# Choice, scores, feature rows and the last LayerNorm of a vision tower moved between its attention loop and its expert loop

## The reference, cut to what matters

```python
h = h + attn(layernorm(h), w_qkv, b_qkv, w_proj, b_proj)      # 32 images x 65 tokens x 64
x = layernorm(h)                                              # "the second LayerNorm"
logits = einsum('bsd,ed->bse', x, gate_w)                     # 64 experts a token
top_logits, indices = top_k(logits, 6)
scores = softmax(top_logits)
xW = einsum('bsd,bskde->bske', x, lattice_weights[indices])
lattice_out = einsum('bske,bsk->bse', xW, scores)
proj = lattice_out @ out_w.T + out_b
y = x + proj
h = h + (y - mean(y)) * rsqrt(var(y) + 1e-5) * ln_g + ln_b
```

## Time and profile before

| what | us |
|---|---|
| median of 3 runs | 1084.4 (1083.52 to 1084.65) |
| the profiled execution | 1083.5 |
| its span in the trace | 1081.6 |
| attention loop, first scores to the end of the last value products | 836.8 to 928.0 |
| from there to the first broadcast of the expert loop | 928.0 to 952.5 |
| expert loop, to the end of the last expert products | 952.5 to about 1070.5 |
| output of the last block | to 1081.6 |

### The profile page before, as it was taken

How to read it: one execution, slowest core, us unless ns; L and a number is a source line. 1 busy time by engine, 2 the same in 40 slices (tenths; PEclk the granted TensorE clock), 3 DMA queues, 4 the chain that set the end, 5 groups by cost and what they waited for, 6 DMA issues and landing times.

```text
span 1081.6 us, 36566 instructions
## 1 busy us (share of the span) xinstructions
PE 979.3 (91%) x17004; PEld 623.9 (58%) x17004; DVE 617.2 (57%) x773; ACT 397.9 (37%) x522; POOL 151.4 (14%) x158
## 2 busy tenths in 40 slices
PE   4899899999989999999899899999899898688885
PEld 3667667657656533676567567656216687533342
DVE  2268457737833221587278357633143677769887
ACT  2432233224223486232332233224675567411100
POOL 6000000000000000000000000020010765334421
PEclk9999999999999899999999999999999899779998
DMA  5220230032022201310220220030001000000000
GB/s 196 93 78 3 69 90 17 3 105 67 4 90 102 59 6 40 109 30 3 93 78 4 78 87 9 4 100 10 14 14 44 2 2 1 2 1 1 2 11 10
DMA packets 25918, 46.78 MB, mean 43 GB/s; under 512 B 9949, under 2 KB 11000, under 8 KB 25125
## 3 DMA queue, kind: packets, MB, share of 16 engines
q1 hardware_dynamic: 24118, 42.47, 12.5%
q0 software_dynamic: 1456, 1.63, 0.6%
q10 hardware_dynamic: 192, 0.33, 0.1%
HBM read 30.25 MB, written 10.89 MB: 38 GB/s over the span
## 4 chain that ended last, share of the span: by engine, by line
PE 74%; DVE 12%; issue 5%; ACT 3%; POOL 3%; DMA 2%; SPq 1%; POOLq 0%; DVEq 0%
PE PSALL L1296 22%; PE PSALL L1264 7%; PE PSALL L1158 5%; PE PSALL L1287 5%; PE PSALL L1373 5%; PE PSALL L1239 4%; PE PSALL L1172 4%; PE PSALL L526 3%; PE PSALL L1383 3%; DVE WORK L1503 3%; PE PSALL L427 2%; DVE WORK L1003 2%; PE PSALL L513 2%; DVE WORK L1522 2%; PE PSALL L1135 2%
## 5 line engine op out<-in xcount | busy, mean ns | idle before, releaser
L1522 DVE STREAM_TRANSPOSE WORK<-PSALL 128x1024 f32<-128x1024 f32 x128 | 152.5, 1230 | 252.9 <-PE PSALL L1264 252.9
L1296 PEld LDWEIGHTS PSALL<-EW,WORK 128*64 128x64 f32 x4096 | 221.8, 138 | 72.8 <-issue 48.3
L1296 PE MATMUL PSALL<-EW,WORK 128*64 128x128 f32 x4096 | 247.6, 276 | 14.0 <-DVE WORK L1522 13.7
L1422 ACT ACTIVATE X<-PSALL,TABLES 128x1024 f32<-128x1024 f32 x128 | 141.8, 1114 | 307.2 <-PE PSALL L1296 307.2
L1503 DVE STREAM_TRANSPOSE WORK<-PSALL 128x1024 f32<-128x1024 f32 x84 | 104.3, 1242 | 32.8 <-PE PSALL L1158 30.9
L324 POOL DMA_DIRECT2D WORK<-MIXED x32 | 17.6, 550 | 670.5 <-ACT MIXED L1413 557.2
L1404 ACT COPY SPEC<-PSALL 128x400 f32<-128x400 f32 x64 | 54.4, 850 | 136.6 <-PE PSALL L1172 132.9
L1172 PEld LDWEIGHTS PSALL<-TABLES,WORK 128*64 128x64 f32 x2000 | 67.1, 138 | 48.8 <-DVE WORK L1503 31.4
L1003 DVE TENSOR_TENSOR WORK<-PSALL,X 128x832 f32<-128x832 f32 x80 | 79.3, 1017 | 16.8 <-PE PSALL L513 15.3
L1172 PE MATMUL PSALL<-TABLES,WORK 128*64 128x64 f32 x2000 | 80.7, 228 | 7.9 <-DVE WORK L1503 3.8
L1456 ACT ACTIVATE WORK<-PSALL,B 128x1024 f32<-128x1024 f32 x64 | 67.8, 1110 | 19.7 <-PE PSALL L1373 19.4
(11 more groups left out here) (157 smaller groups left out, 1157.7 us busy)
## 6 DMA issues: line engine op xcount, KB each, us to landing
SW<-in_spec_w SPq DMA_DIRECT2D x160, 80.0 KB, 2.8
spec_scr<-MIXED SPq DMA_DIRECT2D x24, 400.0 KB, 3.3
SPEC<-spec_scr SPq DMA_DIRECT2D x32, 200.0 KB
WORK<-spec_scr SPq DMA_DIRECT2D x16, 200.0 KB
WORK<-in_coords_w SPq DMA_DIRECT2D x2, 1024.0 KB, 4.8
XC<-in_coords_c SPq DMA_DIRECT2D x2, 1024.0 KB, 7.2
WORK<-MIXED SPq DMA_DIRECT2D x40, 40.0 KB
WORK<-MIXED POOLq DMA_DIRECT2D x32, 40.0 KB
```

Source lines behind the costliest of these rows:

```text
L1296: m = pe.matmul(PS[2 * p + z][64 * j:64 * j + 64, 2 * b * GRID:(2 * b + 2) * GRID], G[:, n % 2, b, h:h + 2, :, t].rearrange("p q o -> p (q ...
L1422: nc.scalar.activation(X[:, n].rearrange("p b (z d) c w -> p d z b (c w)", z=2)[:, p, :, :, 2 * t * GRID:2 * (t + 1) * GRID], PSALL[:, 2 * ...
L1522: nc.vector.transpose(G[:, n % 2, 2 * x + y].rearrange("p h o v -> p o h v"), PSALL[:, 4 + 2 * x:6 + 2 * x, :].rearrange("p k (h o v) -> p ...
```

## The change

- The shared loop ends after step 39 (`TAIL_STEPS` 52 to 40). `ROWS_AT` goes from 26 to 22, `CHOICE_AT` from 32 to 28, `PARTS_AT` from 40 to 37.
- Inside the loop only chunks 0 to 3 get feature rows and logits, at steps 22, 26, 30 and 34 (logits a step later). Chunks 4 to 7 (images 16 to 31) get them in the expert loop, rows at pairs 2, 5, 15 and 18 and logits at pairs 3, 6, 16 and 19, in PSUM banks 6 and 7. DVE waits for the feature rows of a token block before the block's first pair.
- The second LayerNorm (`second_norm`) is one step tighter: its products come at steps 7 and 8 after its start (they were at 9 and 10), its square root at 6 (was 7). For the last block (images 24 to 31) the last four steps are taken between expert pairs 1, 2, 4 and 5; its square root is issued on ACT after `exp_logits(1)`.
- `score_rows(0)` and `score_rows(1)` come one behind the other at step 37, into banks 0, 1 and 2, 3, and so do the parts on ACT and DVE. The low part of chunk 1 is made by DVE, that of chunk 0 still by POOL.
- Behind the loop PE makes four matmuls of 512 columns into bank 5 whose result is not used.
- `PARTS3` lies in `XPS`, and the logits of block k lie one block further on in `LG` (`logits_slot`).
- No DMA is added or removed.

```diff
-ROWS_AT, CHOICE_AT, PARTS_AT = 26, 32, 40
-TAIL_STEPS = 52
+ROWS_AT, CHOICE_AT, PARTS_AT = 22, 28, 37
+TAIL_STEPS = 40
+ROWS_PAIRS = [2, 5, 15, 18]
+NORM_PAIRS = [1, 2, 4, 5]
...
+def part_banks(c):
+
+    return 2 * c if c < 2 else 6
...
-        PARTS3 = sw_mem[:, 0:NT].bitcast(BF16).rearrange("p (g t) -> p g t", g=2)
+        PARTS3 = XPS[:, 0:NT].bitcast(BF16).rearrange("p (g t) -> p g t", g=2)
...
             def gate_rows(c):
...
+                if c < 4:
+                    pe.wait_ge(pj_ready, (ROWS_AT - 5) // BC + c)
+                elif c == 4:
+                    pe.wait_ge(pj_ready, NC)
+                    pe.wait_ge(o_ready, NC)
+                elif c == 6:
+                    pe.wait_ge(rest_ready, 4)
                 if c % 2 == 0:
                     pe.wait_ge(y_ready, LK + c * BC // LB + 1)
...
             def score_rows(c):
...
+                if c < 2:
+                    pe.wait_ge(s_ready, NIMG - 1 + c)
+                elif c == 2:
+                    pe.wait_ge(lg_ready, 6)
+                elif c == 4:
+                    pe.wait_ge(lg_ready, NC)
                 pe.wait_ge(sc_ready, 2 * (c * BC // LB + 1))
-                if c:
+                if c > 2:
                     pe.wait_ge(rest_ready, c)
...
-                if i in (PARTS_AT, PARTS_AT + 2):
-                    score_rows((i - PARTS_AT) // 2)
-
-            pe.wait_ge(gt_ready, NC)
-            pe.wait_ge(lg_ready, NC)
+                if i == PARTS_AT:
+                    score_rows(0)
+                    score_rows(1)
+
+            for i in range(4):
+                pe.matmul(PS[5], ident[:], TABLES[:, :, 0:128], start=True, stop=True)
...
+                if n // 2 in ROWS_PAIRS:
+                    gate_rows(4 + ROWS_PAIRS.index(n // 2))
+                if n // 2 - 1 in ROWS_PAIRS:
+                    gate_logits(4 + ROWS_PAIRS.index(n // 2 - 1))
...
+            gate_rows_out(4)
+            gate_logits_out(4)
             exp_logits(1)
+            deviation(1, LK - 1)
+            gate_rows_out(5)
+            gate_logits_out(5)
...
+                if z == 0:
+                    gate_rows_out(6)
+                    gate_logits_out(6)
...
+                if z == 0:
+                    gate_rows_out(7)
+                    gate_logits_out(7)
...
-                if i in (PARTS_AT + 4, PARTS_AT + 6):
-                    low_part((i - PARTS_AT) // 6)
+                if i == PARTS_AT + 1:
+                    low_part(nc.gpsimd, pool, 0)
...
-                    if i in (PARTS_AT + 2, PARTS_AT + 4):
-                        rest((i - PARTS_AT) // 4)
+                    if i == PARTS_AT:
+                        rest(0)
+                        rest(1)
+                    if i == PARTS_AT + 2:
+                        low_part(nc.vector, dve, 1)
...
+                    if n % PAIRS == 0:
+                        dve.wait_ge(gt_ready, -(-(z + 1) * ZT // CT))
...
+                    if n // 2 in NORM_PAIRS:
+                        second_norm(LK - 1, (4, 5, 7, 8)[NORM_PAIRS.index(n // 2)])
```

More of the change, by code:

```diff
@@ L455, in gate_rows @@
                     pe.wait_ge(lg_ready, c)
-                transposes(c, lambda b: Y[:, b].rearrange("p t d -> p (t d)"), 128, PS[7] if c < 2 else PS[0], gt_full)
+                transposes(c, lambda b: Y[:, b].rearrange("p t d -> p (t d)"), 128, PS[7] if c < 4 else PS[6], gt_full)
             def gate_logits(c):
@@ L491, in tail_tensor @@
                     if i > ROWS_AT:
-                        pe.wait_ge(lg_ready, min((i - ROWS_AT) // BC + 1, 2))
+                        pe.wait_ge(lg_ready, min((i - ROWS_AT) // BC + 1, 4))
                     turn_attended((i - LAG - 2) // BC)
@@ L618, in high_part @@
                 act.wait_ge(st_full, c + 1)
-                nc.scalar.copy(PARTS3[0:3 * EH, :, t], PSALL[0:3 * EH, 6:8, 0:CT]).then_inc(high_ready, 1)
+                nc.scalar.copy(PARTS3[0:3 * EH, :, t], PSALL[0:3 * EH, part_banks(c):part_banks(c) + 2, 0:CT]).then_inc(high_ready, 1)
             def middle_part(c):
@@ L693, in thrice_scores, with low_part @@
                               st[:, 3, a].unsqueeze(2).unsqueeze(3).broadcast_to(thrice), ALU.mult).then_inc(sc_ready, 1)
+        def low_part(ops, eng, c):
+            t = slice(c * CT, (c + 1) * CT)
+            eng.wait_ge(mid_ready, c + 1)
+            ops.tensor_tensor(PARTS3[0:EH, :, t], REST[0:EH, :, t], PARTS3[0:EH, :, t], ALU.subtract).then_inc(lo_ready, 1)
         def tail_pool(pool):
@@ L732, in chosen_scores @@
                                         ).then_inc(weighed, 1)
-            def low_part(c):
-                pool.wait_ge(weighed, c // 2 + 1)
-                t = slice(c * CT, (c + 1) * CT)
-                pool.wait_ge(mid_ready, c + 1)
-                nc.gpsimd.tensor_tensor(PARTS3[0:EH, :, t], REST[0:EH, :, t], PARTS3[0:EH, :, t], ALU.subtract).then_inc(lo_ready, 1)
             pool.wait_ge(nv_ready, NC)
@@ L762, in tail_pool @@
                     weigh_outside(i // BC - 1)
-                if LN_STEP < i < LN_STEP + LK * LB and (i - LN_STEP - 3) % LB == 0:
-                    square(1, (i - LN_STEP - 3) // LB)
+                if LN_STEP < i < LN_STEP + LK * LB and (i - LN_STEP - 2) % LB == 0:
+                    square(1, (i - LN_STEP - 2) // LB)
                 if i == CHOICE_AT + 5:
                     chosen_scores(0)
-                if i in (PARTS_AT + 4, PARTS_AT + 6):
-                    low_part((i - PARTS_AT) // 6)
+                if i == PARTS_AT + 1:
+                    low_part(nc.gpsimd, pool, 0)
             def output_bias(k):
@@ L792, in tail_pool @@
                 residual_and_shift(k - 1)
-                low_part(2 * k)
-                low_part(2 * k + 1)
+                low_part(nc.gpsimd, pool, 2 * k)
+                low_part(nc.gpsimd, pool, 2 * k + 1)
             output_bias(LK - 1)
@@ L973, in tail @@
+                    for k in range(LK):
+                        second_norm(k, i - LN_STEP - k * LB)
                     if i == CHOICE_AT - 1:
                         dve.wait_ge(ho_out.sem, PASSES * ho_out.stride)
-                        link(nc.vector.memset(LG[:, :, EXPERTS:LW], SENTINEL))
+                        link(nc.vector.memset(LG[:, LB:NIMG, EXPERTS:LW], SENTINEL))
+                    if i == NIMG + 1:
+                        link(nc.vector.memset(LG[:, 0:LB, EXPERTS:LW], SENTINEL))
```

105 lines of the change are left out of this document (49 added, 56 removed).

## The result

The changed kernel takes 1087.38 us (median of 12, 1082.46 to 1088.71), the kernel before, in the same runs, 1082.95 us (median of 12). The ratio is 1.0040, with a 95% interval of 1.0023 to 1.0058: 0.4% slower. 1077.0 was forecast, with 1082.5 as the upper end. The profiled execution took 1087.5 us, its span is 1085.5 us.

A forecast was written before the change was run, and what follows sets the result against it. PE bounds attention, DVE the expert loop, and a serial chain through all engines the 24.5 us between. -13.3 + 1.0 + 1.0 + 3.3 + 1.0 - 0.4 = -7.4, from 1084.4 to 1077.0 us; range 1071.5 to 1082.5.

The forecast's parts named there:

- Part 1: Serial stretch from the last value products' end to the first broadcast: 11.2 us instead of 24.5, PE's fillers latest; -13.3.
- T0: End of the last value products in attention, the zero point from which the serial stretch's times are counted.
- Parts 3 to 5: Expert loop: +3.3 for added DVE work, +1.0 for PE's inserted rows and logits, -0.4 for the first broadcast at full clock.
- The stall: Expert loop, pair 4: DVE waits 0.3 us for ACT's square root of the last block's norm.
- the stretched product: Expert loop: one of the norm's two DVE products may meet POOL's product of the chosen scores; +0.4.
- Part 4: PE in the expert loop: four inserted chunks of rows and logits, free at pairs 2 to 6, +1.0 at pairs 15 to 19.
- Part 2: Attention: +1.0 for one more chunk of rows and logits on PE, +1.0 for DVE's lag at steps 28 to 31.
- the extra chunk: Attention, before the last value products end: PE has one more chunk of rows and one of logits, +1.0 in full.
- DVE's lag: Attention, steps 28 to 31: 13.1 us of DVE work against 10.2 to 10.9 of PE, partly absorbed; +1.0, ends 0 and +5.
- A: Rival in attention: DVE becomes the bound, none of the choice work is absorbed, +5 instead of +1, 1081.0; chance 0.18.
- C: Rival: all moved work costs full length, 5 in attention, 5 DVE and 4.1 PE in the loop; +1.4, 1085.8; chance 0.07.
- D: Rival in the expert loop: the clock stays at half through the first token block, PE being too sparse; 1089.6; chance 0.05.

The follow-up runs named there:

- fillers: Changed kernel with six filler matmuls on PE at the end of attention, where it waits; ratio to the kernel before 1.0035.
- after: The changed kernel itself, in its first measurement and profile, against the kernel before; 1087.38 us, ratio 1.0040.
- centre_later: Changed kernel with the second LayerNorm's centring moved one step back to its old place, POOL's squares behind it; ratio to the kernel before 0.9964.
- before_centre_early: Kernel before with only the second LayerNorm's centring and squares moved one step earlier; ratio to the kernel before 1.0044.
- both_later: Changed kernel with the centring one step back and the choice and parts back at steps 32 and 41; ratio to the kernel before 1.0001.
- shifted_between: Changed kernel with centring one step back, and the norm's two products and the shifted logits between masking product and maxima; 1071.8 us, ratio to the kernel before 0.9908.
- after_again: The changed kernel run once more, unaltered, as the level for its group; ratio to the kernel before 1.0058.
- choice_later: Changed kernel with the choice and the parts of images 0 to 7 back at steps 32 and 41; ratio to the kernel before 1.0075.
- square_later: Changed kernel with only POOL's squares of the second LayerNorm one step later, the centring staying early; ratio to the kernel before 1.0033.
- all_between: Changed kernel with the second LayerNorm's early centring and its two products between DVE's masking product and the maxima; ratio to the kernel before 0.9973.

## Why the prediction was wrong

**Part 1 was right** (-13.3 forecast, -13.5 measured), and by its own steps: the data chain ended at T0 + 9.5 (9.1 to 9.9), the fillers at T0 + 11.1 (11.2), and the fillers were what was late. The clock fell at T0 + 2.5, a little before the score rows, and came back at T0 + 9.3 (8.2 to 10.0). With the clock held it is 9.0, the lower end, as `fillers` shows. Two readings behind these bounds were a little off, without consequence: PEclk 0.74 in the slice from 931 puts the fall at 931.5 and not 931.7, and 0.60 in the slice from 958 puts the return at 958.8, 6.3 us after the first broadcast and not 6.0.

**Parts 3 to 5 were nearly right** (+3.9 forecast, +2.8 measured). The stall and the stretched product came as forecast (0.37 for 0.3; 0.35 for 0.4). The table load ahead of that root takes 1.28 us from 961.64 and the root starts at 962.94, again with nothing between. The error is mostly Part 4 (by its own row two inserts of 1.03 us would come to 1.2, not 1.0): PE's four chunks cost nothing that the expert loop shows, where 1.0 was taken. DVE waited 11.0 us for PE in the loop, 2.2 of them before the first pair; before it was 15.3 and 6.6; the rest, 8.8 and 8.7, is level.

**Part 2 failed.** It had +1.0 for the extra chunk and +1.0 for DVE's lag; it was +15.9. The traces, each a single one, split it so:

- 2.3 us lie in the first three images (20.0 us for 17.7), which the change doesn't touch. This is a difference in the clock at the start of attention (13.6 us of half clock from 835 on, 6.8 before) and it varies from run to run; the 1.4 us by which attention began earlier in this execution go the other way.
- 8.9 us (`after` to `centre_later`; 8.4 by `before_centre_early`) are the centring in steps 14, 22 and 30.
- 3.9 us (`centre_later` to `both_later`, and `shifted_between` comes to the same length) are the choice at steps 28 to 31 and the products and shifted logits that meet POOL, in combination: taking away either was enough. This is the lag for which +1.0 was forecast.
- 0.8 us remain for the extra chunk, where 1.0 was forecast.

The failed step is a sentence: "and the tighter norm" was counted as DVE work at steps 28 to 31 alone, and its cost elsewhere at nothing. The prediction gives no reason for that. DVE wasn't short of time there: it was 8.23 of 10 us busy. The instruction itself became more than twice as long in its new place. The same effect was in the forecast, from a row (two products in 3.05 us beside two low parts), and it was applied to the expert loop only. It could have been read for attention: `second_norm` stands behind the maxima in the step, and the maxima are what POOL's 1.05 us subtraction waits for, in every step. The product L970 in the earlier trace rows says that a meeting can take 1649 instead of 682 ns; that one is with a low part, while the products that met the subtraction in before started ahead of it and took 0.68.

The second failing is what follows. A DVE lag of 1 us was costed as 1 us. In the trace it comes out as a PE wait of 1.5 us, and then as half clock: of the 13.6 us from the fourth image on, 7.8 are PE busy time, of which the extra chunk explains 0.7 (`both_later` 69.8, before 69.1).

The Trainium skill, "SBUF — State Buffer", section "Who interferes with whom", covers the longer centring: of a VectorE operation with two SBUF inputs and a GpSimd operation that reads SBUF, the one that starts first keeps the other waiting until it ends. The traces agree, nearly to the sum (0.96 left of L776 and 0.54 after it, where 0.68 is the time alone) and in both orders (the subtraction took 1.50 us at 894.87, behind the product). The Trainium skill excepts in the same place a VectorE operation with at most one SBUF input, and the traces agree there too: the maxima, with one such input, take 0.69 us also where POOL works beside them, as in before at 873.84 (POOL's L716 runs from 873.07 to 874.34).

**The rivals.** A (DVE becomes the bound in attention) had the right place and the wrong price: +5 was its end, made of work and no contention, and it gave 1081.0. C counted everything at full length and took that same 5. D, the only slower one, put the clock's fall in the expert loop; there was no half clock there at all. The clock was the right worry in the wrong stretch. The sign that the prediction gave for being wrong, "if attention grows by more than 5 us", is the one that came true. With the contention taken out of attention (`shifted_between`) the change gives what its stretches add up to, -13.3 + 0.9 + 2.8 = -9.6 us in the trace, and the medians give 1071.8 - 1081.4 = -9.6; the forecast without its lag of DVE was -8.4. And one sentence of the prediction does not hold by its own numbers: all upper ends at once are not C, which keeps Part 1 at -13.3; with the 13.4 us they are +3.6, 1088.0, outside its range.

What stays open is how much of the 8.9 us the clock adds to the waits on average over executions, and why a wait brings the clock down in one place and not in another. Both attempts to hold the clock with extra matmuls left the ratio where it was. What the traces do show: in all six with the centring behind the maxima in its early step (`after`, `after_again`, `choice_later`, `fillers`, `square_later`, `before_centre_early`), PE waits 1.49 us at the first centring and the clock falls within 1.2 us of the end of that wait; in none of the nine with the centring in its late step is there such a fall between 870 and 900. But at the second centring the same wait was followed by a fall in only two of the five changed kernels, and `all_between` had one of 1.47 us at 876.85 without a fall.

## What to carry to other kernels

When an instruction is moved, ask what the other engines do in the microsecond after its new place, and price it from a row where the two meet: DVE work with two SBUF inputs goes ahead of the instruction that releases POOL, or where POOL is idle, and not right behind it; but with too much of it ahead, the release itself comes late (`all_between`). A lag on the engine that feeds a nearly full PE costs more than its length, for the wait that it makes can halve the clock for microseconds after. And a small part that rides along with a large change (here one instruction, one step earlier) deserves its own line in the sum: taken back alone, it turns 0.6% slower into 0.4% faster.

## What the runs showed of the hardware

- Where a 65 x 512 operation on DVE with two SBUF inputs (the centring) starts 0.03 to 0.10 us behind a 65 x 520 subtraction on POOL, it costs DVE 0.87 us (1545 for 679 ns) and POOL nothing (1.05 us). Where DVE starts 0.09 us ahead, DVE loses nothing and POOL 0.45 us (1.50 for 1.05).
- One PE wait of 1.49 us, before 879.84, was followed by half clock; one of 1.49 us before 905.08 in the same trace wasn't, and in `fillers` a slice with no matmul at all (932) stayed at 1.00. Before has a wait of 1.53 us, before 894.24, without a fall. A single trace can't price such a wait.
- Once down in attention, the clock stayed so for 3.4 to 13.7 us in these traces. The code ahead of attention is the same in all kernels, and had between 6.8 and 17.1 us of half clock and a length of 831.1 to 836.8 us. This is why kernels that differ by 4 us in a profile need ten runs.
